# A fused four-block kernel: the second images' causal convolution moved into the projection's matmuls

## What the kernel computes

```
x = x + L0(gn(x))    # depthwise convolutions, a diffusion field, 5 steps
x = x + L1(gn(x))    # 3x3 convolution, 64 to 64 channels
x = x + L2(gn(x))    # layer norm, mamba block, layer norm, projection
x = x + L3(gn(x))    # 2D DCT
```

```
xz = x @ in_proj_w.T
xi, z = split(xz, 2)
xc = causal depthwise convolution of xi, 4 taps, + conv_b
xs = silu(xc)
dt, Bm, Cm = split(xs @ x_proj_w.T)
delta = softplus(dt @ dt_proj_w.T + dt_proj_b)
h_t = exp(delta_t * A) * h_(t-1) + delta_t * xs_t * B_t     # 16 states
y_t = sum over states of h_t * C_t, + xs_t * D
y = y * silu(z);  out = y @ out_proj_w.T
```

## Time and profile before

| what | value |
| --- | --- |
| scan instructions, L1775 | 128, 290.4 us on DVE |
| scan inputs, L1766 | 70, 84.8 us on DVE |
| states times C, L397 | 127, 299.9 us on POOL |
| convolution multiply-adds, L1730 | 24 of 1281 ns |
| convolution products, L1727 | 8 |
| chain that ended last | DVE 31%, PE 30%, ACT 20%, issue 13% |

### The profile page before, as it was taken

One profiled execution on the slowest core, in us unless ns is written; L12 is line 12 of the kernel. 1 busy time (PEld: TensorE's weight loads), 2 busy tenths in 40 slices (PEclk: granted clock), 3 DMA queues, 4 the chain that ended last, 5 costly groups with the idle time before them and its releaser, 6 DMA issues.

```text
span 897.5 us, 10547 instructions
## 1 busy us (share of the span) xinstructions
PE 729.4 (81%) x3866; PEld 499.1 (56%) x3866; DVE 792.5 (88%) x682; ACT 560.2 (62%) x960; POOL 519.5 (58%) x243
## 2 busy tenths in 40 slices
PE   3898898977777678788799789988768677878896
PEld 2343343443677567778654434434338566777783
DVE  6979997769999998999969989775999999989984
ACT  2973342237669898979486724223684977897932
POOL 3104997121489697778510299912047979878851
PEclk9999999999789999999999999999988999999999
DMA  4002000000635355355200210000033445545431
GB/s 114 0 15 80 0 1 0 0 1 6 184 123 185 139 179 189 137 188 184 75 1 0 75 43 0 0 1 1 0 106 131 159 160 186 194 157 186 157 105 24
DMA packets 34066, 78.20 MB, mean 87 GB/s; under 512 B 15704, under 2 KB 15840, under 8 KB 34016
## 3 DMA queue, kind: packets, MB, share of 16 engines
q1 hardware_dynamic: 32608, 76.23, 25.3%
q0 software_dynamic: 320, 1.05, 0.5%
q10 hardware_dynamic: 1088, 0.26, 0.1%
HBM read 70.71 MB, written 2.62 MB: 82 GB/s over the span
## 4 chain that ended last, share of the span: by engine, by line
DVE 31%; PE 30%; ACT 20%; issue 13%; POOL 2%; DMA 1%; SPq 1%; DVEq 0%; POOLq 0%; ACTq 0%
ACT arena L958 15%; PE ps L749 7%; PE ps L510 6%; DVE arena L1775 6%; DVE ps L1766 5%; PE ps L549 4%; DVE HS L1775 3%; DVE arena L1730 3%; PE ps L763 2%; PE ps L641 2%; ACT ROWS L958 1%; ACT ps L958 1%; PE ps L600 1%; POOL arena L397 1%; PE ps L663 1%
## 5 line engine op out<-in xcount | busy, mean ns | idle before, releaser
L397 POOL TENSOR_TENSOR arena<-arena 128x1024 f32<-128x1024 f32 x85 | 200.3, 2368 | 60.9 <-DVE arena L1775 55.1
L958 ACT ACTIVATE arena<-arena 128x128 f32<-128x128 f32 (+3 forms) x412 | 157.0, 455 | 82.4 <-DVE arena L1669 64.7
L1775 DVE TENSOR_TENSOR_SCAN arena<-arena,ps 128x1024 f32<-128x1024 f32 x86 | 194.7, 2277 | 10.6 <-ACT arena L958 5.7
L958 ACT ACTIVATE arena<-arena,Amat 128x1024 f32<-128x1024 f32 x128 | 143.0, 1142 | 7.2 <-DVE arena L1775 6.0
L641 PE MATMUL ps<-mat,arena 128*128 128x128 f32 x1016 | 138.1, 281 | 5.5 <-POOL arena L397 5.0
L600 PE MATMUL ps<-mat,arena 128*128 128x128 f32 x560 | 82.2, 295 | 61.9 <-DVE arena L1775 35.9
L641 PEld LDWEIGHTS ps<-mat,arena 128*128 128x128 f32 x1016 | 119.7, 146 | 9.5 <-POOL arena L397 7.5
L397 POOL TENSOR_TENSOR arena<-HS,arena 128x1024 f32<-128x1024 f32 x42 | 99.6, 2370 | 30.1 <-DVE HS L1775 21.5
L749 PE MATMUL ps<-arena,mat 128*128 128x512 f32 x240 | 106.9, 595 | 9.4 <-DVE arena L1642 9.4
L600 PEld LDWEIGHTS ps<-mat,arena 128*128 128x128 f32 x560 | 66.8, 148 | 76.2 <-DVE arena L1775 45.3
L1775 DVE TENSOR_TENSOR_SCAN HS<-arena,ps 128x1024 f32<-128x1024 f32 x42 | 95.7, 2277 | 2.4 <-ACT arena L958 1.7
(11 more groups left out here) (219 smaller groups left out, 1321.8 us busy)
## 6 DMA issues: line engine op xcount, KB each, us to landing
arena<-c_rows SPq DMA_DIRECT2D x128, 512.0 KB, 3.9
arena<-arena SPq DMA_DIRECT2D x16, 252.0 KB
out<-arena SPq DMA_DIRECT2D x28, 64.0 KB, 2.4
xres<-x POOLq DMA_DIRECT2D x4, 256.0 KB, 5.4
xres<-x SPq DMA_DIRECT2D x4, 256.0 KB, 4.1
convw<-conv_w SPq DMA_DIRECT2D x1, 576.0 KB
c_rows<-ROWS SPq DMA_DIRECT2D x4, 128.0 KB, 1.9
mat<-mats SPq DMA_DIRECT2D x1, 448.0 KB, 3.9
```

The source lines that it names most:

```text
L397: tt(HC[s % 2], HS[s % 3], CB[s % 4], ALU.mult).then_inc(S("hc"), 1)
L958: return nc.scalar.activation(out_, in_, func, bias=bias, scale=scale, accum_out=accum_out)
L1775: nc.vector.tensor_tensor_scan(HS[s % 3], DA[s % 3], PS[q][:, :], 0.0, ALU.mult, ALU.add).then_inc(S("scan"), 1)
```

## The change

The convolution of each pair's second image (b = 1) leaves DVE. It is linear, so it is put in front of the projection: with both = [x_t ; x_(t-1)], the second image's 64 normalized channels and the same ones one column later on the other 64 partitions, one matmul with 128 weight rows does two taps, and a second one on columns shifted by two does the other two. The weights tapw are in_proj_w times the tap's factor, made once on POOL; the factors are spread over the partitions by a matmul of ones with diagonal matrices (PE), copied to ROWS by ACT. Two DMAs per pair and half fill `both` (D[k]["W1"]) from XNC.

Besides, relu_part moves from POOL to DVE for tiles 1 to 3 (for tile 3 still in the scan, right behind one_plus(3)), and the orders of PE, ACT and DVE change in the head of the scan. The core of the diff:

```diff
+        tapw = sb("tapw", 2 * P)
 # SP
+            def shifted_copies(h, k):
+                here, both = D[k]["XNC"][C:P, :], D[k]["W1"]
+                sp.wait_ge(S("xnc"), 2 * h + k + 1)
+                sp.wait_ge(S("first_column"), h + 1)
+                sp.dma_start(both[0:C, :], here).then_inc(S(f"shift{k}"), 16)
+                sp.dma_start(both[C:P, 1:L], here[:, 0:L - 1]).then_inc(S(f"shift{k}"), 16)
             for h in range(HALVES):
+                for k in range(2):
+                    shifted_copies(h, k)
                 store_rows(h, 0)
 # POOL
+            pool.wait_ge(S("tap_rows"), 2)
+            pool.wait_ge(S("bn_rstd"), 7)
+            for tap in range(4):
+                part = slice(C * (tap % 2), C * (tap % 2) + C)
+                if tap > 0:
+                    pool.wait_ge(S("tapw"), tap)
+                tt(blk(tapw, tap // 2)[part, :], inw[part, 2 * P * (tap % 2):2 * P * (tap % 2) + P], blk(ROWS, 3 - tap)[part, :],
+                   ALU.mult).then_inc(S("tapw"), 1)
+            pool.wait_ge(S("tapw"), 4)
...
                 for k in range(2):
+                    last = pool.memset(D[k]["W1"][:, 0:1], 0.0)
+                last.then_inc(S("first_column"), 1)
...
-                relu_part(h, 1)
-                relu_part(h, 2)
                 for s in range(SCANS):
...
-                    if s == 5:
-                        relu_part(h, 3)
 # PE
+            pe.wait_ge(S("tap_diag"), 5)
+            mm(half(PS[3], 1), blk(ROWS, 0), half(ROWS, 1), start=True, stop=True).then_inc(S("tap_rows"), 1)
...
+            def x_convolved(h, k):
+                both, ps = D[k]["W1"], x_ps(k, 1)
+                pe.wait_ge(S("tapw"), 4)
+                pe.wait_ge(S("first_column"), h + 1)
+                pe.wait_ge(S(f"shift{k}"), 32 * h + 32)
+                pe.wait_ge(S(f"sz{k}"), 2 * h + 1)
+                for n in range(2):
+                    c0, c1 = n * BANK, n * BANK + BANK
+                    first = max(c0, 2)
+                    mm(ps[:, c0:c1], blk(tapw, 0), both[:, c0:c1], start=True, stop=False, skip_group_check=True)
+                    last = mm(ps[:, first:c1], blk(tapw, 1), both[:, first - 2:c1 - 2], start=False, stop=True, skip_group_check=True)
+                last.then_inc(S(f"xi{k}"), 1)
...
-                x_in_proj(h, 0, 0)
+                x_in_proj(h, 0)
                 z_in_proj(h, 0, 0)
-                x_in_proj(h, 0, 1)
+                x_convolved(h, 0)
                 xn_channels(h, 1)
                 dt_proj(h, 0, 0)
-                x_in_proj(h, 1, 0)
+                x_in_proj(h, 1)
+                dt_proj(h, 0, 1)
                 z_in_proj(h, 1, 0)
-                dt_proj(h, 0, 1)
-                x_in_proj(h, 1, 1)
+                z_in_proj(h, 0, 1)
+                z_in_proj(h, 1, 1)
+                x_convolved(h, 1)
+                bc_proj(h, 0)
                 dt_proj(h, 1, 0)
-                z_in_proj(h, 0, 1)
-                bc_proj(h, 0)
                 turn_first_rows(h)
...
-                z_in_proj(h, 1, 1)
                 dt_proj(h, 1, 1)
 # ACT
+            act.wait_ge(S("tap_rows"), 1)
+            av(half(ROWS, 0), half(PS[3], 1), ACT.Identity).then_inc(S("tap_rows"), 1)
...
                 silu_z(h, 0, 0)
                 silu_x(h, 0, 0)
+                silu_x(h, 0, 1)
                 layer_scale(h, 1)
                 abs_x(h, 0, 0)
-                silu_x(h, 0, 1)
+                abs_x(h, 0, 1)
                 silu_z(h, 1, 0)
-                abs_x(h, 0, 1)
                 silu_x(h, 1, 0)
+                silu_z(h, 0, 1)
+                silu_z(h, 1, 1)
+                silu_x(h, 1, 1)
                 exp_of(h, 0)
                 exp_of(h, 1)
-                silu_z(h, 0, 1)
+                keep_rows(h, 0)
                 abs_x(h, 1, 0)
                 exp_of(h, 2)
-                keep_rows(h, 0)
                 ln_of(h, 0)
-                ln_of(h, 1)
                 keep_first_b(h)
-                ln_of(h, 2)
-                silu_x(h, 1, 1)
-                silu_z(h, 1, 1)
+                for j in range(1, 3):
+                    ln_of(h, j)
                 decay(h, 0)
 # DVE
+            dve.memset(blk(ROWS, 0), 1.0).then_inc(S("tap_diag"), 1)
+            for t in range(4):
+                ts(blk(ROWS, 4 + t), ident, vecs[:, V_CONVW + t:V_CONVW + t + 1], None, ALU.mult).then_inc(S("tap_diag"), 1)
...
-                causal(h, 0, 0, rest=False)
+                causal(h, 0, range(1))
                 variance(1, h, 0)
-                causal(h, 0, 0, first=False)
+                causal(h, 0, range(1, 4))
                 normalize(1, h, 0)
-                causal(h, 0, 1)
-                causal(h, 1, 0)
                 relu_x(h, 0, 0)
+                causal(h, 1, range(4))
                 relu_x(h, 0, 1)
-                causal(h, 1, 1)
                 one_plus(h, 0)
                 one_plus(h, 1)
-                first_relu_part(h)
+                relu_part(h, 0)
+                relu_part(h, 1)
                 relu_x(h, 1, 0)
                 one_plus(h, 2)
+                relu_part(h, 2)
                 delta(h, 0)
...
                 one_plus(h, 3)
+                relu_part(h, 3)
```

More of the change, by code:

```diff
@@ L560, in xn_channels, with x_in_proj @@
                 transposes(D[k]["XN"], PS[2 * k + 1]).then_inc(S("xnT"), 1)
-            def x_in_proj(h, k, b):
+            def x_in_proj(h, k):
                 pe.wait_ge(S("xnc"), 2 * h + k + 1)
-                if b == 1:
-                    pe.wait_ge(S(f"sz{k}"), 2 * h + b)
                 for n in range(2):
-                    last = mm(half(x_ps(k, b), n), inw[:, 2 * P * b:2 * P * b + P], half(D[k]["XNC"], n), start=True, stop=True)
+                    last = mm(half(x_ps(k, 0), n), inw[:, 0:P], half(D[k]["XNC"], n), start=True, stop=True)
+                last.then_inc(S(f"xi{k}"), 1)
[10 more added lines that the diff above has]
+                    last = mm(ps[:, first:c1], blk(tapw, 1), both[:, first - 2:c1 - 2], start=False, stop=True, skip_group_check=True)
                 last.then_inc(S(f"xi{k}"), 1)
@@ L571, in z_in_proj @@
                 pe.wait_ge(S("xnc"), 2 * h + k + 1)
-                if b == 1:
-                    pe.wait_ge(S(f"rx{k}"), 2 * h + b)
+                if b == 1 and k == 0:
+                    pe.wait_ge(S("rx0"), 2 * h + 1)
+                if b == 1 and k == 1:
+                    pe.wait_ge(S("cconv1"), 4 * h + 4)
                 wz = inw[:, 2 * P * b + P:2 * P * b + 2 * P]
@@ L581, in dt_proj @@
                 pe.wait_ge(S(f"xs{k}"), i + 1)
+                if k == 1 and b == 0:
+                    pe.wait_ge(S("sz1"), 2 * h + 2)
                 project(x_ps(k, b), dtw[:, :], D[k]["XS"][:, b * L:b * L + L]).then_inc(S(f"dt{k}"), 1)
@@ L587, in bc_proj @@
                 pe.wait_ge(S(f"sz{k}"), 2 * h + 2)
+                if k == 1:
+                    pe.wait_ge(S("rx1"), 2 * h + 1)
                 for n in range(2):
@@ L711, in _ @@
                 pe.wait_ge(S(f"group{k}"), g_var(0, 0))
+                if k == 1:
+                    pe.wait_ge(S("tap_rows"), 2)
                 write_all(PS[2 * k + 1])
@@ L1078, in silu_x @@
             def silu_x(h, k, b):
-                i = 2 * h + b
-                act.wait_ge(S(f"cconv{k}"), 4 * i + 4)
-                av(D[k]["XS"][:, b * L:b * L + L], D[k]["XI"], ACT.Silu, 1.0, vc("m_conv_b")).then_inc(S(f"xs{k}"), 1)
+                if b == 0:
+                    act.wait_ge(S(f"cconv{k}"), 4 * h + 4)
+                else:
+                    act.wait_ge(S(f"xi{k}"), 2 * h + 2)
+                convolved = D[k]["XI"] if b == 0 else x_ps(k, 1)[:, :]
+                av(D[k]["XS"][:, b * L:b * L + L], convolved, ACT.Silu, 1.0, vc("m_conv_b")).then_inc(S(f"xs{k}"), 1)
             def abs_x(h, k, b):
@@ L1718, in x2_norm, with causal @@
                 group_norm(D[k], h, 2, k)
-            def causal(h, k, b, first=True, rest=True):
-                d, i = D[k], 2 * h + b
-                dve.wait_ge(S(f"xi{k}"), i + 1)
-                if b == 1:
-                    dve.wait_ge(S(f"xs{k}"), i)
-                w = [vecs[:, V_CONVW + t:V_CONVW + t + 1] for t in range(4)]
-                if first:
-                    ts(d["XI"], x_ps(k, b)[:, :], w[3], None, ALU.mult).then_inc(S(f"cconv{k}"), 1)
-                for t in range(1, 4) if rest else []:
-                    dve.wait_ge(S(f"cconv{k}"), 4 * i + t)
-                    stt(d["XI"][:, t:L], x_ps(k, b)[:, 0:L - t], w[3 - t], d["XI"][:, t:L], ALU.mult, ALU.add)\
-                        .then_inc(S(f"cconv{k}"), 1)
+            def causal(h, k, some):
+                d = D[k]
+                w = [vecs[:, V_CONVW + t:V_CONVW + t + 1] for t in range(4)]
+                for t in some:
+                    if t == 0:
+                        dve.wait_ge(S(f"xi{k}"), 2 * h + 1)
+                        ts(d["XI"], x_ps(k, 0)[:, :], w[3], None, ALU.mult).then_inc(S(f"cconv{k}"), 1)
```

(14 more changed lines are left out.)

18 lines of the change are left out of this document (2 added, 16 removed).

## The result

The changed kernel takes 908.11 us in the median of four runs (907.65 to 908.73), the kernel before 901.11 in the median of its four (899.17 to 903.37). The ratio is 1.0074, 95% interval 1.0054 to 1.0093: slower, by 7.0 us. The forecast was 910.5 (range 903.5 to 914.5). The profiled execution has a span of 906.3 us against 897.5, 8.8 more; it took 908.06 us, and that of before 899.3.

The account below looks back on a forecast made before the run. DVE was taken to set the pace before, with exp(0) behind TensorE's chain holding it up afterwards. 1.7 + (0.6 - 0.6 + 3.3) + (1.6 - 0.6 + 3.3) = +9.3 us: 908.6 profiled, 910.5 as median, range 903.5 to 914.5.

Parts of the forecast that it names:

- The start, 1.7: Kernel setup: DVE's memset and four products add 1.2 us, ACT's extra copy 0.5, all on the path.
- One_plus(0), +0.6 and +1.6: Head of the scan: one_plus(0) starts 0.6 us later in the first half, 1.6 in the second, waiting for exp(0).
- the clock that the prediction spoke of: First half of the kernel before: dt's matmuls took 3.27 us at a mean granted clock of 0.72, called a dip.
- From there to the scan, -0.6 and -0.6: One_plus(0) to first scan, each half: DVE gains subtractions, +2.3 and +0.1, but products without POOL's turns save 3.0.
- The subtraction in the scan, +3.3 twice: Tile 3's subtraction, moved to DVE behind the softplus step, waits for POOL's product: +3.3 us per half.
- The shifted copies and pair 0's extra pass, 0: Second half's head: copies land in 5 us, in time; x_convolved's four matmuls end before transposes that wait for DVE; cost 0.
- so 1.9 goes on top at the end: Conversion from profiled execution, 899.3 us, to median of runs, 901.2: 1.9 us added, making 908.6 into 910.5.
- The range's lower end, 903.5: Fast end of the predicted range, described as B with C and a cheaper start.
- B: Rival, in the scan: order tips and tile 3's subtraction costs 1.4 us instead of 3.3; 906.7 us, chance 0.15.
- C: Rival, in the scan: POOL's freed 2.4 us at s = 5 pull sums in, -4.8 in both halves; 905.7, chance 0.08.
- A: Rival, head of the scan: DVE's stream still sets the time, one_plus(0) follows the last relu; -6.5, 894.7 us, chance 0.07.
- D: Rival, at z(1,1): PE falls to the 1.2 GHz clock, 1.4 us per event; one per half gives 913.3, chance 0.15.

Follow-up runs that it names:

- e5: Kernel before with only the tile 3 subtraction moved from POOL to DVE, right behind one_plus(3): 907.70 us, ratio to before 1.0076.
- e7: Changed kernel with pair 1's x_convolved cut to its first pass, two matmuls of 512 columns less per half: 903.58 us, ratio to before 1.0039.
- e8: Changed kernel with pair 0's x_convolved cut to its first pass, the older two taps left out: one execution, 909.98 us, only its stages read.
- e3: Changed kernel with exp(0) and exp(1) right behind abs_x(0, 1) on ACT and z(1, 1) made behind bc_proj(0): 901.70 us, ratio to before 0.9995.
- e1: Changed kernel with the tile 3 subtraction back on POOL, after its product of step 5: 902.37 us, ratio to before 1.0015.
- e6: Changed kernel with the tile 3 subtraction still on DVE but two instructions later, right behind scan_step(3): 904.23 us, ratio to before 1.0031.
- e9: Changed kernel with the subtraction on POOL, setup work moved later, early exp(0) and exp(1), and TensorE and ACT reordered: 895.44 us, ratio to before 0.9940.

## Why the prediction came out as it did

- **The start, 1.7.** Measured in the trace: first statistics at 16.97 against 15.98, so 1.0; as DVE's setup happened to begin 0.3 us earlier in this execution, the work costs 1.3. This term was sized 0.4 too high: the four products take 0.74 us together, not the 1.08 worked out from the earlier trace rows. (The other executions lie around that: 16.79 to 17.33 with the changed setup, 15.59 in e5, which has that of before.) ACT's copy costs the 0.5 forecast (15.36 to 15.85).
- **One_plus(0), +0.6 and +1.6.** 20.85 against 20.21 and 19.20: +0.64 and +1.65. e7 shows that the chain over x_convolved(1) sets it and e8 that pair 0's doesn't; e3 shows that exp(0) is what DVE waits for. The 1.0 us between the two halves of before goes with the clock that the prediction spoke of; its row, which the earlier trace rows should have held, is this window of the kernel before (granted clock third from last):

```profile
200.00:206.00 6.00, 6.00 (x18) 2.98 (x17) 4.97 (x5) 3.47 (x3) 0.00 (x0) 0.72 0.00 0
```

e5, whose instructions up to there are those of before, was granted 1.00 in that window and took 19.20 in the first half too. So the +0.64 of the first half is +1.65 in an execution of before without the dip: that the forecast's +0.6 came out rests on both readings being of the one execution that had it.

- **From there to the scan, -0.6 and -0.6.** 17.25 against 17.86 and 17.26 against 17.84. The product behind delta(0) fell from 3.26 to 1.23 (667.56), as POOL had nothing left there.
- **The subtraction in the scan, +3.3 twice.** 16.19 and 16.17 against 12.88. e1 and e5 take it away and add it alone; e6 shows that it is the turn with POOL, and that the one that issues first has it. The Trainium skill ("SBUF — State Buffer", "Who interferes with whom") says that a DVE instruction with two SBUF inputs and a GpSimd instruction that reads SBUF exclude each other, and that the order of issue decides who blocks. The trace agrees: 3.25 us behind one_plus(3), 1.20 behind a scan step.
- **The shifted copies and pair 0's extra pass, 0.** Right. The copies landed 2.9 and 3.7 us after their issue, so the 5 us of the prediction was too much, and nothing hung on it; for the extra pass, e8.
- **The sum.** 1.0 + 0.6 - 0.6 + 3.3 + 1.65 - 0.6 + 3.3 = 8.7, the span's difference is 8.8, and 9.3 was forecast. That these two agree to 0.1 is luck in part: the first half's scan was 1.0 us shorter than in before and the stretch between the halves 1.0 longer, and neither was forecast. By medians it is 7.0. The step that failed is the last and plainest one, "so 1.9 goes on top at the end". The profiled execution of before took 899.3, at the fast end of its four timed ones (899.17 to 903.37), and that of the changed kernel sits in the middle of its own (908.06, median 908.11). An offset of one kernel's draw is no constant of the measurement; without it the forecast would have read 908.6. The 55 runs of before that stood beside the experiments spread from 898.3 to 903.6 around 901. A part of that goes with the clock: the 17 with a mean granted clock of 0.951 or less have a median of 902.8 us, the 14 with 0.961 or more one of 900.3; the profiled execution of before had 0.967, that of the changed kernel 0.954. This was not tried by itself, and why the medians lie 1.7 us closer than the stages add up to stays open.
- **What the slowdown is made of, by timed runs.** The subtraction of tile 3 alone makes 6.9 us in the kernel before (e5) and 5.7 in the changed one (e1), and with it undone the changed kernel is 1.0015 of before. So most of the 7.0 us is this one instruction. All the rest of the change, the convolution that left DVE and its setup included, costs 1.4 us by e1's ratio and 2.1 by the stages.
- **Rivals.** The range's lower end, 903.5, is not the sum that it is said to be: B and C together give 910.5 - 3.8 - 4.8 = 901.9. A (DVE's stream goes on setting the time) is refuted by the 7.96 us hole and by e3. B (the subtraction costs 1.4) by the table. C (POOL's freed time pays something back) by 188.10 against 188.12 in the second half; in the first half the spread of that stage, with and without POOL's subtraction (e8 190.84 without, e9 190.06 with), hides anything under 1 us. D (a clock drop at z(1, 1)) didn't happen in the changed kernel: the granted clock was 1.00 from 210 to 217 and from 646 to 652 us. Its like is seen where PE waits 3.4 us in that stretch, before x_convolved(1) in e3's first half and before dt_proj(1, 0) in e9 (0.64 from 212 to 216 us, 0.55 from 643 to 647).
